# Who adds the last bias: VectorE in every group, or GpSimd in every second one

## What is computed

```python
slot = jnp.where(keep, idx.astype(jnp.int32) * cap + loc, E * cap)
disp = jnp.zeros((E * cap, D), x.dtype).at[slot].set(xf, mode='drop')
...
h = jnp.einsum('ecd,edf->ecf', disp, w1) + b1[:, None, :]
y = (jnp.einsum('ecf,efd->ecd', h, w2) + b2[:, None, :]).reshape(E * cap, D)
out = jnp.where(keep[:, None], gate_val[:, None] * y[jnp.minimum(slot, E * cap - 1)], 0.0)
...
y2 = _ln(y1 + _moe(y1, wg, w1, b1, w2, b2), ln2_g, ln2_b)
```

## Time and profile before

| | us |
|---|---|
| median of 3 runs | 2509.3 |
| lowest and highest of them | 2507.39, 2509.95 |
| the profiled execution, its time | 2509.4 |
| its span in the profile | 2507.7 |
| first to last result scatter, first expert stage | 533.93 to 649.07 |
| the same, second expert stage | 2384.30 to 2499.44 |

### The profile page before, as it was taken

One profiled execution on the slowest core, in us unless ns is written; L12 is line 12 of the kernel. 1 busy time (PEld: TensorE's weight loads), 2 busy tenths in 40 slices (PEclk: granted clock), 3 DMA queues, 4 the chain that ended last, 5 costly groups with the idle time before them and its releaser, 6 DMA issues. The chain is left out here.

```text
span 2507.7 us, 47389 instructions
## 1 busy us (share of the span) xinstructions
PE 2231.7 (89%) x15250; PEld 1330.2 (53%) x15252; DVE 1929.4 (77%) x5490; ACT 1569.3 (63%) x3207; POOL 919.2 (37%) x1158
## 2 busy tenths in 40 slices
PE   6999997977389889999999999999987999998474
PEld 4666666866155534444444444444465666666363
DVE  4677776589598788889888898998845677776496
ACT  2555554256144459999999999999941455554263
POOL 1577787036354400000000000000011387777166
PEclk7999998998699979999999999999998999999796
DMA  4233252856268424454444444444245122322673
GB/s 119 77 122 114 86 200 95 282 190 194 84 203 208 143 56 95 94 96 93 93 89 89 96 93 95 96 93 88 46 134 177 34 85 85 102 104 71 217 225 101
DMA packets 233752, 298.79 MB, mean 119 GB/s; under 512 B 43150, under 2 KB 181457, under 8 KB 232867
## 3 DMA queue, kind: packets, MB, share of 16 engines
q1 hardware_dynamic: 206483, 235.82, 36.8%
q0 software_dynamic: 17152, 50.49, 5.3%
q10 hardware_dynamic: 9872, 9.45, 1.2%
HBM read 203.36 MB, written 100.60 MB: 121 GB/s over the span
## 5 line engine op out<-in xcount | busy, mean ns | idle before, releaser
L2288 DVE CUSTOM_DVE_ANT_0 banks<-banks,ahead_bias 128x128 f32<-128x128 f32 (+7 forms) x1024 | 760.4, 776 | 94.1 <-PE banks L1997 80.5
L2203 ACT ACTIVATE attn_probT<-banks 128x512 f32<-128x512 f32 x1152 | 623.0, 608 | 72.3 <-PE banks L2014 61.8
L1997 PE MATMUL banks<-ahead_kst,ahead_qst 96*128 96x512 bf16 (+3 forms) x1536 | 425.9, 337 | 12.1 <-DVE attn_low L2288 7.4
L2014 PE MATMUL banks<-ahead_qst,ahead_kst 99*128 99x256 bf16 (+3 forms) x2176 | 394.9, 280 | 6.7 <-ACT banks L2194 1.3
L2345 POOL CAST attn_lowp<-attn_lowT 128x32 bf16<-128x32 f32 x64 | 13.4, 209 | 848.1 <-DVE attn_lowT L2296 848.1
L2036 PE MATMUL banks<-attn_probT,ahead_vb 128*32 128x256 f32 (+3 forms) x4352 | 315.6, 400 | 8.8 <-ACT attn_probT L2203 8.3
L2194 ACT COPY banks<-ahead_biasT 128x512 f32<-128x512 f32 x480 | 281.2, 611 | 16.3 <-PE banks L2052 6.6
L1997 PEld LDWEIGHTS banks<-ahead_kst,ahead_qst 96*128 96x128 bf16 x1536 | 118.9, 97 | 264.5 <-DVE attn_low L2288 174.3
L2014 PEld LDWEIGHTS banks<-ahead_qst,ahead_kst 99*128 99x128 bf16 x2176 | 180.8, 98 | 140.4 <-ACT attn_probT L2203 43.5
L438 PE MATMUL banks<-ffn_xT,winT 128*128 128x512 f32 x512 | 250.6, 613 | 4.6 <-DVE ffn_w L756 1.7
L977 POOL TENSOR_TENSOR ffn_w1T<-ffn_ring,own 128x512 f32<-128x512 f32 x128 | 134.4, 1062 | 176.5 <-PE banks L475 102.6
(11 more groups left out here) (259 smaller groups left out, 3955.3 us busy)
## 6 DMA issues: line engine op xcount, KB each, us to landing
ffn_ring<-disp SPq DMA_DIRECT2D x144, 257.0 KB, 3.2
ahead_qst<-qparts SPq DMA_DIRECT2D x384, 64.0 KB, 2.8
ahead_kst<-kparts SPq DMA_DIRECT2D x192, 128.0 KB, 5.0
ffn_ring<-in_L_attn_x_dram SPq DMA_DIRECT2D x32, 512.0 KB, 5.1
ffn_w<-in_L_ffn_w_dram SPq DMA_DIRECT2D x16, 1024.0 KB, 9.3
ahead_bias<-neard SPq DMA_DIRECT2D x128, 128.0 KB, 2.2
ahead_biasT<-neardT SPq DMA_DIRECT2D x128, 128.0 KB, 5.7
ffn_ring<-x SPq DMA_DIRECT2D x32, 512.0 KB, 4.9
```

The costliest lines, as they stand in the source:

```text
L1997: mm = nc.tensor.matmul(score[k % 2][:, a:e], qst[0:K6, u, half, hh, ii * P:(ii + 1) * P], kst[0:K6, u, hh, a:e], start=True, stop=True)
L2014: mm = nc.tensor.matmul(tbank[t % 3][:, at:at + nb * P], kst[:, u, hh, j * P:(j + 1) * P], qst[:, u, half, hh, x:x + nb * P], start=(k == ...
L2203: nc.scalar.activation(probT[:, g % 2, i, 0:w], tbank[t % 3][:, 0:w], ACT.Exp, scale=-1.0).then_inc(s_exp, 1)
L2288: nc.vector.tensor_tensor_reduce(out=part, in0=part, in1=bias[:, hh, T - w:T], scale=1.0, scalar=BIG, op0=ALU.add, op1=ALU.min, accum_out= ...
```

## The change

In groups with an odd number VectorE stops after the multiplication, and GpSimd waits for that (`s_scaled`), does the addition itself, waits for its own result (`s_added`, a new semaphore) and then scatters. In groups with an even number all is as it was; `s_fin` now counts these alone. Nothing else moves, and the values computed are the same.

```diff
@@ GpSimd, expert stage
             for n in range(GROUPS):
-                pool.wait_ge(s_fin, n + 1)
+                if n % 2:
+                    pool.wait_ge(s_scaled, n + 1)
+                    nc.gpsimd.tensor_tensor(all_rows(n, 0, C), all_rows(n, 0, C), all_rows(n, C, 2 * C), ALU.add
+                                            ).then_inc(s_added, 1)
+                    pool.wait_ge(s_added, n // 2 + 1)
+                else:
+                    pool.wait_ge(s_fin, n // 2 + 1)
                 pool.wait_ge(s_inv, n + 1)
@@ VectorE, scale(n)
-                dve.wait_ge(s_scaled, n + 1)
-                nc.vector.tensor_tensor(all_rows(n, 0, C), all_rows(n, 0, C), all_rows(n, C, 2 * C), ALU.add).then_inc(s_fin, 1)
+                if n % 2 == 0:
+                    dve.wait_ge(s_scaled, n + 1)
+                    nc.vector.tensor_tensor(all_rows(n, 0, C), all_rows(n, 0, C), all_rows(n, C, 2 * C), ALU.add).then_inc(s_fin, 1)
```

More of the change, by code:

```diff
@@ L1087, in ffn @@
         s_got = [ph.sem("got0"), ph.sem("got1")]
-        s_tps, s_tsb, s_zps, s_sum, s_st, s_mv, s_ve, s_sd, s_inv2, s_rs, s_norm, s_scaled, s_fin, s_marked, s_seed, s_inv, s_fac = (
-            ph.sem(x) for x in ("tps", "tsb", "zps", "sum", "st", "mv", "ve", "sd", "inv2", "rs", "norm", "scaled", "fin",
+        s_tps, s_tsb, s_zps, s_sum, s_st, s_mv, s_ve, s_sd, s_inv2, s_rs, s_norm, s_scaled, s_added, s_fin, s_marked, s_seed, s_inv, s_fac = (
+            ph.sem(x) for x in ("tps", "tsb", "zps", "sum", "st", "mv", "ve", "sd", "inv2", "rs", "norm", "scaled", "added", "fin",
                                 "marked", "seed", "inv", "fac"))
```

## The result

| | before | after |
|---|---|---|
| median of the runs, us | 2509.6 (2507.4 to 2510.9) | 2539.5 (2537.0 to 2540.4) |
| ratio after / before | | 1.0116 [1.0100, 1.0132] |
| span of the profiled execution, us | 2507.7 | 2538.7 |
| first, second expert stage (first scatter to the end of the last), us | 115.1, 115.1 | 131.2, 132.1 |

The changed kernel is slower, as forecast, but by 30 us where 9.4 were forecast, and 2539.5 lies above the range's end of 2530. Both stages grew, by 16.1 and 16.9 us; the rest of the span lost 2. The figures in this part are those of the profiled executions.

The account below looks back on a forecast made before the run. Each expert stage was taken to last until GpSimd's last scatter, with GpSimd pacing after the change: pairs of 12.48 + 0.87 = 13.35 us, two stages 9.4 us longer, 2509.4 + 9.4 = 2518.8, so 2519 us; range 2506 to 2530.

Parts of the forecast that it names:

- VectorE's own hold: VectorE at tiny L1521, ahead of L1526: held to the add's end, about 1.3 us a pair, at no cost.
- one of my signs of being wrong: Expert stages: GpSimd waiting for VectorE in mid-stage would show the forecast wrong; no size given.
- VectorE's pair without the addition: VectorE, an even and an odd group: 13.31 us less 1.25 for the addition leaves 12.06 us.
- TensorE late by 0.6 at that length: TensorE's product ahead of VectorE's sums: would come 0.6 us late should the pair fall to 12.06 us.
- GpSimd's own pair: GpSimd, two groups: eight scatters, seven gaps, the add up to the next scatter and a longer first scatter, 12.48 us.
- Scatters held for 0.87 a pair: Odd group's first scatter on GpSimd: held to the end of VectorE's L1526, 0.87 us per pair.
- the forecast's 119.9: Length of one expert stage in us: 9 x 13.35 - 0.30, which is 4.7 more than 115.14.
- The stage as nine like pairs: Expert stage: eighteen groups taken as nine equal pairs of 13.35 us on GpSimd, less the last gap of 0.30.
- Edits at nothing: SyncE's ring refills keep 3 us of room; the extra semaphore is one more clear of 38 ns; both counted at nothing.
- The miss: Expert stages: adds meet only sums and statistics, no scatter starts under L1526 or L1529; 2503.2 us, chance 0.10.
- the partial miss: Expert stages: holds of 0.07 to 0.62 us a pair leave the time within 5 us, near 2509; chance 0.16.
- Piled holds: Expert stages: the add or more scatters held too, 1.5 us a pair, +10.4 us a stage, 2530 us; chance 0.08.

Follow-up runs that it names:

- the last experiment: Changed kernel, adds also awaiting VectorE's small operations, even group's fourth scatter issued between add and its wait: nine adds 2519.3 us (1.0049), five adds 2504.6 us (0.9986).
- the first experiment: Changed kernel with one more wait: GpSimd's add starts only after VectorE's small operation L1496 of the same body; 2525.3 us, ratio 1.0059.

## Why the prediction was wrong in size, and right in sign

**The step that failed** is the sentence that VectorE's own hold "costs nothing: it only takes VectorE's lead away", with the place given for it, L1521. It rests on an order that never comes about. I let GpSimd fall behind first (its 13.35 against VectorE's 12.06), so that the add would fall where VectorE has time to spare, with a hold of 1.3 us at L1521 (there is none: L1527 takes 0.16 throughout). But in the first odd group GpSimd isn't behind: it is in the scatter just ahead of the add when L1532 ends, the add is due at once, and L1496, next on VectorE, stands from 539.72 for 3.10 us. That costs VectorE 2.93 where it has saved 1.25, so VectorE stays the later engine (14.97 against GpSimd's 13.0 and its holds), GpSimd has caught up by the next pair, and the same meeting comes again. The hold sustains itself, seven times a stage; one of my signs of being wrong, GpSimd waiting for VectorE in mid-stage, is what came. The added wait breaks it, and all that I had said about the pair then comes true in outline: GpSimd paces, and VectorE is held in the tiny operations for free.

**Terms, one by one.**

- VectorE's pair without the addition, 13.31 - 1.25 = 12.06: right, 12.06 without an add. TensorE late by 0.6 at that length: right, 12.7 in some pairs.
- GpSimd's own pair, 12.48: too short, 13.06 measured. The add takes 2.38 and not the 2.18 of the earlier trace rows (its own time and no hold: 2.36 at 658.19, with VectorE done), and the next scatter starts 0.78 after it and not 0.16. The 0.16 was a misreading of the earlier trace rows. In the program the scatters L967 that follow L952 belong to the group before and don't wait for it, while the moved add's scatters wait for their add; the last experiment has 0.16 without such a wait, where the kernels with it have 0.78. The waits did not "stand in the 2.34 us".
- Scatters held for 0.87 a pair: the sum is right where GpSimd paces, 0.57 + 0.28 = 0.85, but in two scatters and not in one, so part of it is luck. With the right own time the pair would have been 13.91 and nine of them 125, 124.3 measured in the first experiment; the forecast would have been 2509.4 + 2 x (124.9 - 115.1) = 2529 for a kernel in which GpSimd paces; the first experiment took 2525.
- The kernel nearest to the one that I priced is the last experiment's with nine adds: GpSimd's own pair is 13.06 - 0.62 = 12.44 there, and the stages of 120.2 and 119.3 stand beside the forecast's 119.9. Its adds follow each other in 12.7 to 13.7 us for the most part and not in 13.35 each, so the likeness of the totals is partly chance.
- The stage as nine like pairs: nearly right where GpSimd paces. In the changed kernel it is two regimes: VectorE paces through seven holds, worth 10.0 + 1.7 us, and then comes an end with two adds at GpSimd's pace, worth 4.4.
- Edits at nothing (SyncE's ring loads, the extra semaphore): nothing in the profile after speaks against them. The span outside the stages is 2 us shorter, which I did not follow up.

**The rivals.** The miss and the partial miss did not occur in the changed kernel; but the miss can be *made*, and 0.9956 is its outcome with five adds. Piled holds (2530) was nearest in size and wrong in mechanism: it, too, had GpSimd pace. What I lacked was the rival in which VectorE, held on its own path, stays the bound: 13.31 - 1.25 + 2.2 = 14.3 with the add of the earlier trace rows, 6 us a stage over six pairs, and the end of the stage beside it. How long the hold lasts (2.93 and not 2.2) was not to be read before. What speaks for it could be read before: GpSimd waits 1.18 us for VectorE in the groups of the earlier trace rows, so a moved add goes off at once, and in the program the small operations on SBUF follow straight on the multiplication.

**The account** in the time of the program: the 18 additions leave VectorE, -17; the holds at L1496, with the interface taken early, +14; GpSimd's own time, with the adds at the stages' ends, the remaining +33. These three are differences of runs (no add, nine adds with the wait, nine without); the last also holds the scatters' holds, and is not split further.

## What to carry to other kernels

When work moves to an engine that shares an interface with the one it came from, look first at what the relieved engine does in the microseconds after the signal that starts the moved work; a 4-element operation there can cost the whole length of the moved one. If the signal falls badly, let the moved work wait for a later semaphore, so that it lies beside operations that don't need the shared side (here sums from PSUM and statistics): one wait was worth 14 to 19 us. Then move only as much as the receiving engine has room for without pacing, and nothing where it already paces (the end of the stage): five groups gave -11.5 us, nine with the same wait +16.

## What I had not expected of the hardware

- An operation of 4 elements a partition is held to the end of the other engine's operation like a large one: 3.10 us at L1496 for 0.17 us of work; the multiplication L1532 at 645.04, met by the add of 644.90, takes 3.31 for 1.22.
- GpSimd's add held VectorE 0.7 to 0.8 us before its shown start, under a running scatter (3.10 against 2.29 us with GpSimd idle). A start in the profile's rows is then no safe sign of when the hold begins.
- CAST and TENSOR_SCALAR on 128x4, each with one operand in SBUF, are held too (1.86 and 2.02 us by an add), the latter also by a memset that reads nothing (2.07). RECIPROCAL on 128x4 was not, in the places where it met an add (0.17).
- Between the end of a GpSimd add and the start of the scatter that waits for it lie 0.78 us, against 0.30 between scatters; it was the same behind a memset, and 0.16 where the scatter doesn't wait for the add.
